# Late row tiles in five buffers, a fifth group buffer, and a new order of the first groups in a graph network with routed experts

## What is computed

```python
def rgcn_gate_layer(x, row, col, edge_type, basis, att, gate_w, root, bias):
    w = jnp.einsum('rb,bio->rio', att, basis)
    x_j = x[col]
    msgs = []
    for r in range(NUM_RELATIONS):
        gate = jax.nn.sigmoid(x_j @ gate_w[r, :, 0])
        msgs.append(gate[:, None] * x_j @ w[r])
    msg = jnp.where((edge_type == 0)[:, None], msgs[0], msgs[1])
    agg = jax.ops.segment_sum(msg, row, num_segments=x.shape[0])
    return agg + x @ root + bias

h = relu(layer1(layernorm(x)));  x = x + layer2(h)          # z is layer2(h)
t = layernorm(x)
shared = sum over 2 experts of gelu(t @ sw1.T + sb1) @ sw2.T + sb2
probs = softmax(t @ gate_w.T + gate_b); the two largest of 8 weigh the routed experts
x = x + shared + routed
```

## Time and profile before

| | us |
|---|---|
| median of 3 runs (lowest, highest) | 1658.48 (1655.58, 1662.76) |
| the profiled execution | 1659.22 |
| its span, first to last instruction | 1657.5 |
| PE, DVE, ACT, POOL busy | 1498.5, 929.2, 707.3, 660.3 |
| mean granted clock | 0.965 |

### The profile page before, as it was taken

One profiled execution on the slowest core, in us unless ns is written; L12 is line 12 of the kernel. 1 busy time (PEld: TensorE's weight loads), 2 busy tenths in 40 slices (PEclk: granted clock), 3 DMA queues, 4 the chain that ended last, 5 costly groups with the idle time before them and its releaser, 6 DMA issues. The chain is left out here.

```text
span 1657.5 us, 27765 instructions
## 1 busy us (share of the span) xinstructions
PE 1498.5 (90%) x8680; PEld 1203.4 (73%) x8680; DVE 929.2 (56%) x2663; ACT 707.3 (43%) x1230; POOL 660.3 (40%) x989
## 2 busy tenths in 40 slices
PE   6999899979997999999999774399999999999997
PEld 4777666767785777777888652288787888788886
DVE  5555676957732333346665356366666666664453
ACT  3334335656631111124665333255555555453232
POOL 3762232467742000002666334254545454533222
PEclk9999999999999999999999985699999999999999
DMA  9999999687759999996776885657676766434220
GB/s 245 275 281 285 292 304 302 188 242 132 130 69 264 286 279 288 279 287 193 131 132 120 198 170 156 188 160 217 182 221 175 222 180 210 150 121 136 101 71 5
DMA packets 130212, 325.95 MB, mean 197 GB/s; under 512 B 17115, under 2 KB 17641, under 8 KB 129698
## 3 DMA queue, kind: packets, MB, share of 16 engines
q1 hardware_dynamic: 84626, 211.19, 43.2%
q0 software_dynamic: 45456, 113.12, 30.1%
HBM read 205.62 MB, written 121.74 MB: 198 GB/s over the span
## 5 line engine op out<-in xcount | busy, mean ns | idle before, releaser
L1186 ACT ACTIVATE th<-bank 128x512 fp32r<-128x512 f32 x158 | 94.3, 597 | 297.5 <-PE bank L1450 281.1
L985 POOL DMA_INDIRECT gx<-y,dst_slot x42 | 45.5, 1083 | 271.5 <-ACT xn_e L1206 251.3
L1430 PE MATMUL bank<-root2h,th 128*128 128x512 f32 x316 | 133.9, 424 | 19.4 <-DVE tl L1796 14.4
L1796 DVE SCALAR_TENSOR_TENSOR tl<-bank,th 128x512 fp32r<-128x512 f32 x79 | 54.4, 690 | 163.9 <-ACT th L1186 163.9
L1119 POOL DMA_INDIRECT out<-xt,out_row x90 | 93.4, 1038 | 132.5 <-DVE xt L2149 103.1
L1430 PE MATMUL bank<-root1h,th 128*128 128x512 f32 x316 | 131.8, 417 | 8.0 <-DVE yout L1825 5.3
L1825 DVE TENSOR_TENSOR yout<-bank,bias_b 128x512 f32<-128x512 f32 x152 | 103.9, 683 | 61.6 <-DMA z<-yout 35.4
L1430 PE MATMUL bank<-root2l,th 128*128 128x512 f32 x316 | 126.2, 399 | 0.0
L1430 PE MATMUL bank<-root2h,tl 128*128 128x512 f32 x316 | 125.9, 398 | 0.0
L1430 PE MATMUL bank<-root1l,th 128*128 128x512 f32 x316 | 125.0, 396 | 0.0
L1430 PE MATMUL bank<-root1h,tl 128*128 128x512 f32 x316 | 124.5, 394 | 0.0
(11 more groups left out here) (334 smaller groups left out, 4375.8 us busy)
## 6 DMA issues: line engine op xcount, KB each, us to landing
basis_t<-in_gnn_basis SPq DMA_DIRECT2D x64, 896.0 KB
xt<-sorted_rows SPq DMA_DIRECT2D x45, 560.0 KB, 3.9
xin<-in_x SPq DMA_DIRECT2D x39, 512.0 KB
xin<-y SPq DMA_DIRECT2D x39, 512.0 KB
y<-yout SPq DMA_DIRECT2D x37, 512.0 KB
z<-yout SPq DMA_DIRECT2D x34, 512.0 KB
stage0q<-in_x SPq DMA_DIRECT2D x5, 1024.0 KB
stage1q<-in_x SPq DMA_DIRECT2D x5, 1024.0 KB, 8.8
```

Source lines behind the costliest of these rows:

```text
L985: pool.indirect_dma_start(out=gx[:, e % 6, :], out_offset=None, in_=x if pr.phase == SB else y1, in_offset=bass.IndirectOffsetOnAxis(ap=ds ...
L1186: act.activation(th_a[:, s, :], tpb[s][:], f).then_inc(s_hi, 1)
L1430: ins = pe.matmul(out_ap, a(k), b(k), start=first, stop=last)
L1796: ins = dve.scalar_tensor_tensor(out=tl_a[:, s, :], in0=tpb[s][:], scalar=0.0, in1=th_a[:, s, :].bitcast(F32), op0=ALU.max, op1=ALU.subtract)
```

## The change

Five pairs of late rows have five buffers (`late_last` is new), so none is used twice, and the transfers that add them to z go to slots 1 to 6 on POOL (`add_late_rows`); `y_out` no longer waits for them. SP loads the up-projection weights ahead of groups 0 and 1. A fifth group buffer, `stage4q`, lies where tiles 2 and 3 lie later; group q of 5 and up uses buffer (q - 1) % 4. Therefore `load_tile(2)` waits for group 4's sort as well, and `load_group(4)` only for the last transpose of the late tiles. The split of the biases moves from behind group 3 to late tiles 0 and 1 on DVE. PE, ACT, DVE and POOL take groups 0 to 4 in a new order, and group 4 comes ahead of tile 0. Functions that only changed `stage[q % 4]` to `stage_of(q)` are left out here.

```diff
@@ -232,6 +232,7 @@
         late_out, _ = place("late_out", [P, 2, H], at=m_at)
+        late_last, _ = place("late_last", [P, 2, H], at=m_at - 8 * H)
...
@@ -283,6 +283,9 @@
         xt3, x5 = place("xt3", [P, 2, XW], at=x4)
+        stage4q, x6 = place("stage4q", [P, QT, XW], at=x3)
+        assert x6 == x5
+        stage = (stage0q, stage1q, stage2q, stage3q, stage4q)
...
@@ -541,18 +544,31 @@
-            k = (g - NC // 2) % 4
-            return (yout[:, k % 2, :, :], k) if k < 2 else ((xn_a, late_out)[k - 2][:, :, :], k)
+            k = g - NC // 2
+            return (yout[:, k, :, :], k) if k < 2 else ((xn_a, late_out, late_last)[k - 2][:, :, :], k)
...
         def late2_added(eng):
-            for k in range(5):
-                eng.wait_ge(s_late2[k], 16 * (len(LATE2_PAIRS[k::4]) if k < 4 else 1))
+            for k in range(6):
+                eng.wait_ge(s_late2[k], 16)
...
             return st.t.i is None and st.t.k == NT - 1
...
+        def stage_of(q):
...
+            return stage[q if q < LEAD_GROUPS else (q - 1) % 4]
...
+        def stage_free(eng, q):
...
+            if q == LEAD_GROUPS - 1:
+                eng.wait_ge(s_tp, 2 * (NT + ET))
+            elif LEAD_GROUPS <= q < LEAD_GROUPS + 4:
+                eng.wait_ge(s_sorted[q - LEAD_GROUPS], 16 * QT)
+            else:
+                wait(eng, s_sorted[q % 4], 16 * QT * (q // 4))
...
@@ -827,16 +843,13 @@
             sp.wait_ge(s_mm, E0)
+            load_up_experts()
...
             load_group(1)
-            load_up_experts()
...
                 load_pair(SE, Pos(g))
-                if g < NG:
-                    load_group(2)
-                else:
-                    load_group(3)
+                load_group(g - NC // 2 - 2)
...
@@ -844,6 +857,7 @@
             load_group(7)
+            sp.wait_ge(s_sorted[0], 16 * QT * 2)
...
@@ -1120,31 +1134,30 @@
+            def add_late_rows(k):
+                if k < len(LATE2_PAIRS):
+                    add_late2(LATE2_PAIRS[k])
+                else:
+                    pool.wait_ge(s_y, 2 * NT)
+                    pool.dma_start(z[TAIL + again:N, :], scratch[again:P, :], accum_op=ALU.add).then_inc(s_late2[-1], 16)
...
                 add_z(q)
-            add_late2(LATE2_PAIRS[0])
-            add_late2(LATE2_PAIRS[1])
-            group_rstd(0)
-            group_extras(0)
-            add_late2(LATE2_PAIRS[2])
-            add_late2(LATE2_PAIRS[3])
-            group_rstd(1)
-            group_extras(1)
-            group_rstd(2)
-            group_extras(2)
-            add_late2(LATE2_PAIRS[4])
-            group_rstd(3)
-            group_extras(3)
-            pool.wait_ge(s_y, 2 * NT)
-            pool.dma_start(z[TAIL + again:N, :], scratch[again:P, :], accum_op=ALU.add).then_inc(s_late2[-1], 16)
             for q in range(4):
-                sort_rows(q)
-                if q:
-                    add_z(q + 3)
+                if q == 3:
+                    add_z(4)
+                group_rstd(q)
+                group_extras(q)
+            sort_rows(0)
...
             group_extras(4)
+            sort_rows(1)
+            add_z(5)
+            sort_rows(2)
+            group_rstd(5)
+            sort_rows(3)
+            add_z(6)
             rows_of_tile(0)
-            group_rstd(5)
...
@@ -1159,6 +1172,8 @@
                     group_rstd(group_at(i, 11))
+                if 0 < i <= len(LATE2_PAIRS) + 1:
+                    add_late_rows(i - 1)
...
@@ -1304,11 +1319,14 @@
-            def q_norm(q):
+            def q_norm(q, js=range(QT)):
                 s = q % 2
-                act.wait_ge(s_qst, q + 1)
-                for j in range(tiles_of(q)):
-                    rows = stage[q % 4][:, j, 0:H]
+                if js[0] == 0:
+                    act.wait_ge(s_qst, q + 1)
+                for j in js:
+                    if j >= tiles_of(q):
+                        continue
+                    rows = stage_of(q)[:, j, 0:H]
...
@@ -1371,25 +1389,28 @@
                     expert_hi(FC + i - 2)
-                if i == LAST_E - 2:
-                    q_norm(0)
-                    for k in range(KC):
-                        q_full(0, k)
-            q_logits(0)
+            q_norm(0)
+            for k in range(KC):
+                q_full(0, k)
             for q in range(1, 4):
-                q_norm(q)
-                q_exp(q - 1)
+                q_norm(q, range(2))
+                if q > 1:
+                    q_exp(q - 2)
+                q_norm(q, range(2, QT))
+                q_logits(q - 1)
...
                     q_full(q, k)
-                q_logits(q)
+            q_exp(2)
+            q_logits(3)
+            q_norm(4, range(2))
             q_exp(3)
-            q_norm(4)
+            q_norm(4, range(2, QT))
+            for k in range(KC):
+                q_full(4, k)
+            q_logits(4)
...
             f_shares(0)
-            for k in range(KC):
-                q_full(4, k)
-            q_logits(4)
...
@@ -1663,26 +1684,29 @@
-            for e in range(LAST_E - 1):
+            for e in range(LAST_E + 1):
...
             turn_group(0)
-            late2_step(LAST_E - 1)
...
             logits(0)
-            logits_by_token(0)
-            late2_step(LAST_E)
             for q in range(1, 4):
-                turn_group(q)
+                q_transpose(q, 0)
+                q_transpose(q, 1)
+                logits_by_token(q - 1)
+                if q > 1:
+                    count_ranks(q - 2)
+                q_transpose(q, 2)
+                q_transpose(q, 3)
                 logits(q)
-                logits_by_token(q)
-                count_ranks(q - 1)
+            logits_by_token(3)
+            count_ranks(2)
+            turn_group(4)
+            logits(4)
             count_ranks(3)
+            logits_by_token(4)
...
                 turn_tile(0, part)
-            turn_group(4)
-            logits(4)
-            logits_by_token(4)
...
@@ -1808,9 +1832,7 @@
                 apart = is_tail(st)
-                if st.phase == SE and st.g.k - 4 in LATE2_PAIRS and not apart:
-                    dve.wait_ge(s_late2[0], 16)
-                elif st.t.mod(2) == 0 and not apart and (st.phase != SE or late2_buffer(st.g.k)[1] < 2):
+                if st.t.mod(2) == 0 and not apart and (st.phase != SE or late2_buffer(st.g.k)[1] < 2):
...
@@ -1994,30 +2016,35 @@
                 for k in range(2):
-                    dve.tensor_copy(b1r[:, 4 + 2 * k:6 + 2 * k, :], halves[:, k, :, :].bitcast(F32))
+                    ins = dve.tensor_copy(b1r[:, 4 + 2 * k:6 + 2 * k, :], halves[:, k, :, :].bitcast(F32))
+                link(ins)
...
+            def down_bias_rows():
...
+            def row_columns(t):
+                dve.memset(t[:, :, H:SHARES], 0.0)
+                link(dve.memset(t[:, :, SHARES:XW], 0.0))
+                for k in range(2):
+                    ins = dve.memset(t[:, :, SHARES + k * NR2 + NE:SHARES + (k + 1) * NR2], 1.0)
+                return ins
...
             def router_tiles():
-                scattered(dve, 1)
-                dve.wait_ge(s_sm2, 16 * (3 + 2 + 5))
...
                 dve.memset(is_kind[:], 0.0)
+                for t in stage[0:4]:
+                    row_columns(t)
...
+            def gate_tiles():
+                scattered(dve, 1)
                 dve.memset(topv[:], 3.0e38)
-                dve.memset(gwp[:, :, NE:32], 0.0)
-                for t in stage:
-                    dve.memset(t[:, :, H:SHARES], 0.0)
-                for t in stage:
-                    ins = dve.memset(t[:, :, SHARES:XW], 0.0)
-                link(ins)
-                dve.tensor_copy(gwp[:, :, 0:NE], gw[:])
-                for t, k in itertools.product(stage, range(2)):
-                    ins = dve.memset(t[:, :, SHARES + k * NR2 + NE:SHARES + (k + 1) * NR2], 1.0)
-                ins.then_inc(s_qs, 1)
+                link(dve.memset(gwp[:, :, NE:32], 0.0))
+                dve.tensor_copy(gwp[:, :, 0:NE], gw[:]).then_inc(s_qs, 1)
...
@@ -2158,21 +2185,29 @@
                     expert_lo(FC + e - 2)
-                if e == 5:
+                if e == 0:
+                    up_bias_rows()
+                if e == 1:
+                    down_bias_rows()
+                if e == 4:
                     router_tiles()
-                if e == 6:
+                if e == 8:
+                    gate_tiles()
                     q_stats(0, range(QT))
-                if e == 8:
+                if e == 9:
                     q_stats(1, range(QT))
+            dve.wait_ge(s_tp, 2 * (NT + ET))
+            row_columns(stage4q).then_inc(s_qs, 1)
...
             route_a(0)
+            q_stats(3, range(QT))
...
             sort_kinds(0)
-            q_stats(3, range(QT))
...
             sort_kinds(1)
+            q_stats(4, range(QT))
...
@@ -2182,15 +2217,13 @@
             sort_kinds(3)
-            bias_rows()
+            q_stats(5, range(QT))
...
```

(9 more changed lines are left out.)

28 lines of the change are left out of this document (13 added, 15 removed).

## The result

| | before | after |
|---|---|---|
| median of 4 runs each (lowest, highest), us | 1657.49 (1655.58, 1662.76) | 1617.97 (1612.88, 1620.96) |
| the profiled execution, us | 1659.22 | 1620.96 |
| its span, us | 1657.5 | 1619.2 |
| mean granted clock | 0.965 | 0.981 |

The ratio is 0.9753, 95% interval 0.9719 to 0.9788: 35 to 47 us faster. The forecast was 1624, its range 1608 to 1645.

The account below looks back on a forecast made before the run. Bound taken: some 71 us of idle TensorE between 900 and 1100 us, from waits in the engines' fixed orders. Gains of 39.9 less 5.5 given back make 34.4: 1659.2 to 1624.8, 0.7 less for the median, 1624; range 1608 to 1645.

Parts of the forecast that it names:

- first marker: First bias matmul of slot 0 on TensorE; forecast at 1036.0 instead of 1069.56, 33.6 us gained.
- Late rows: Late tiles on VectorE: ninth output at 965, group 0 2.2 us later, group 1 normalised at 977.5, 11 us earlier.
- four places that lose time: ScalarE's 6.84 us for weights, VectorE's 13.35 for yout, 10.0 per serial group, group 4's 28.69 for its statistics.
- wait (b): VectorE stands 13.35 us before reusing yout, because the first late rows' add to z takes 23.75 us to land.
- The overlapped groups: Logits and turn back beside the next normalising: 7 us per group instead of 10.0; positions of group 2 at 1005.3, 22.8 gained.
- the low clock through the groups: Rival: TensorE stays at 1.2 GHz, 9 to 9.5 us per group, 6 to 8 us less gain, 1631; chance 0.14.
- From positions to tile 0: Group 2's positions to tile 0's turn: 19.5 us as now plus 5.5 for a late sort start; turned at 1030.3.
- Group 4: With its own buffer finished near 1011, ahead of tile 0; 5.7 us from tile 0's turn to slot 0's first bias matmul.
- Slot 0: First regular tile slot: 13.5 us instead of 19.8, as group 4's count and group 5 come earlier; 6.3 us gained.
- what is given back: Losses in the slots: tile 2 late 2.5 us, tile 1 about 1, clock 1.5, late adds 0.5; together 5.5.
- my sign of being wrong: Slots 1 to 6 longer than 13.5 us would show the forecast wrong.
- the rival of free transfers: Transfers don't slow each other: x of group 5 5 us earlier, tiles 1 and 2 unwaited, 8.5 more gain, 1616; chance 0.10.

Follow-up runs that it names:

- the run with the serial groups: Changed kernel with groups 1 to 3 back in the old one-after-the-other order on TensorE and ScalarE, all else kept: 1618.98 us.
- kernel with late buffers and weights: Kernel before with only the five late-row buffers, their adds in slots 1 to 6, and the up-projection weights loaded ahead of groups 0 and 1: 1653.46 us.
- the kernel with the busy TensorE: Changed kernel with 76 more identity transposes on TensorE between group 4's turn back and tile 0: 1615.24 us.

## Why the prediction was right, and where it was not

| step | forecast | profile after |
|---|---|---|
| ninth late output | 965 | 966.2 |
| group 1, group 3 normalised | 977.5, 991.5 | 978.9, 994.6 |
| positions of group 2 | 1005.3 | 1009.4 |
| tile 0 turned | 1030.3 | 1028.1 |
| first marker | 1036.0 | 1034.3 |
| second marker | about 1051 (1052 by the sum's terms) | 1053.1 |
| gain, net | 34.4 | 36.5, and 1.8 behind it |

The sum was right, and so was the mechanism as a whole; several terms were not.

*Late rows.* Right: 3.3 us for the bias work (3.0 by its undoing), group 1 at 977.5. Wrong was to take the weights as one of four places that lose time: alone and with the late buffers their move gave nothing. The 6.84 us lay beside the wait for z of group 0, whose add follows the last messages of the edges, and only the new order made them count. In the forecast they stand in the same step as wait (b), which hid this.

*The overlapped groups.* The pitch of 7 was 7.8 (978.92 to 994.57); VectorE's 3.11 us for z of group 2, which landed 21.0 us after its issue, lie in it, and the forecast had no such wait. The 7 us a group were carried whole into tile 0. The run with the serial groups shows that this link was false: 3.8 us in the positions, nothing at tile 0 (it is turned 1.8 us later with the overlap), 1.1 us at the third marker. In the kernel before the positions set the sort's start; once they come early, x of group 5 does. I had that wait in the sum, as 5.5 us, without drawing the conclusion that the overlap then buys nothing. By the same argument the low clock through the groups (6 to 8 us less gain) would have cost little; that was not tried.

*From positions to tile 0.* This term was mis-sized most: 25.0 forecast, 18.7 measured. The sort started 3.8 behind the positions instead of 5.8 (0.3 now and 5.5 more), its issues ended at 1018.7, and landing and load took 9.4 us from there, instead of the 13.3 that I had kept from the kernel before. It hid the 4.1 us by which the positions were late: two errors of opposite sign, and luck in the sum.

*Group 4.* Right in kind: 5.7 to the marker forecast, 6.2 measured. Undoing the buffer costs 14.5 us at the third marker. The kernel with late buffers and weights has 160.5, the changed one with its buffer undone 143.3: 17.2 us come from the rest of the change, chiefly its order (all late tiles ahead of group 0, group 4 ahead of tile 0). At the normalising of group 3 the profiles divide the lead: it comes 71.4 us behind the first late output in the kernel with late buffers and weights, 62.9 with the serial groups and the late tiles ahead of them, 58.1 in the changed kernel. So 8.5 us there, net of the bias work, come with the late tiles ahead of group 0, which no longer stand between the statistics of groups 0, 1 and 2 on VectorE, and 4.9 with the overlap. How much of each reaches the third marker no run divides, apart from the overlap's 1.1; that stays open.

*Slot 0.* 13.5 and what is given back, some 16 to the second marker, forecast; 18.8 measured. The first products took 5.7 us, 2.7 more than at full clock, where I took 1.5 and had 2.7 as the bound; tile 1 waited 2.94 instead of 1; tile 2 did not wait, where I had 2.5. These terms were added up as if they lay in series: what slot 0 loses on the clock and on tile 1 also gives tile 2 the time to land. Slots 1 to 5 took 67.4 us with the late adds and 67.8 before the change; three of them were over 13.5, my sign of being wrong, but so were three in the kernel before, so that sign could not tell anything.

The Trainium skill's page "DMA: Bandwidth & Descriptors" gave, by its section "Anatomy of one DMA — SWDGE (gpsimd) path", an estimate of 4.4 us for x of a group. The trace has 6.67 for x of group 5, issued at 1004.08 with group 1's sort beside it: between the page and the 11.13 that I took. That section is on transfers that GpSimd issues, and x is issued by SyncE. By my own terms x at 1004.1 would also have taken 4.0 us off the sum, rather than the 5 that I gave, as GpSimd was ready only at 1006. And the 11.13 us came with sorts and an add under way, as I wrote there, not "beside little else", as I wrote against the rival of free transfers. The landing at 1010.8 agreed with my 1010 only because it was also issued 4.4 us later than I had worked out.

## What to carry to other kernels

When a buffer is what a group waits for, one more buffer moves the wait to the next user of the old one; price the change by when that one arrives, and count no gain that would have to arrive sooner. Before adding up stops, ask of each what else lands at the same time: of the four that I listed, the weights were worth nothing in the kernel before, and the serial order of the groups almost nothing in the changed one. Where several transfers are in flight, don't price an earlier issue at its full worth: in the one order tried here a sort issued 4.0 us sooner brought its tile 0.6 us. And before a long transfer is taken for its own price, look what was issued just ahead of it.

## What the runs showed of the hardware

The same load of a tile from sorted_rows took 3.70 us in the changed kernel, where an x load and a sort were issued behind it, and 8.06 where a z add and a sort were issued ahead of it and an x load behind it. Of four z adds issued 0.8 us apart the first landed after 8.5 us and the last after 25.3. And filling TensorE's stop of some 11 us with transposes did not keep the clock: it was 0.97 in the filled stretch, at its upper level for the turn of tile 0, and fell to the lower one 4.5 us after that turn began, behind a stop of 2.35 us; the stretches of the kernel with the busy TensorE (granted clock third from the end):

```profile
1010.00:1020.00 10.00, 8.79 (x81) 7.57 (x81) 4.54 (x20) 1.88 (x3) 4.54 (x7) 0.97 0.81 211
1020.00:1030.00 10.00, 6.83 (x50) 6.37 (x49) 5.79 (x36) 5.59 (x9) 6.57 (x11) 0.88 0.88 282
1030.00:1040.00 10.00, 6.96 (x52) 6.58 (x52) 3.18 (x10) 4.03 (x8) 4.25 (x5) 0.84 1.05 281
```
